# A graph network's second layer: where the split between gathered tiles and weighed blocks stands

## The reference, cut to what matters

```python
def _gcn_conv(x, edge_index, edge_weight, W, b):
    deg = segment_sum(w, col);  dinv = rsqrt(deg)
    norm = dinv[row] * w * dinv[col]
    h = x @ W
    msg = h[row] * norm[:, None]
    return segment_sum(msg, col) + b
x = x + relu(_gcn_conv(h, ...))
```

## Time and profile before

| | us |
|---|---|
| median of 3 runs | 1101.44 (1101.41 to 1103.09) |
| the profiled execution | 1098.35 |
| its span, first to last instruction | 1096.6 |
| layer 2's steps on DVE, in the span | 329.6 to 565.2 |
| busy in the span: PE, DVE, POOL, ACT | 928.3, 827.0, 586.4, 449.9 |

### The profile page before, as it was taken

One profiled execution on the slowest core, in us unless ns is written; L12 is line 12 of the kernel. 1 busy time (PEld: TensorE's weight loads), 2 busy tenths in 40 slices (PEclk: granted clock), 3 DMA queues, 4 the chain that ended last, 5 costly groups with the idle time before them and its releaser, 6 DMA issues.

```text
span 1096.6 us, 23929 instructions
## 1 busy us (share of the span) xinstructions
PE 928.3 (85%) x6145; PEld 587.6 (54%) x6145; DVE 827.0 (75%) x2605; ACT 449.9 (41%) x887; POOL 586.4 (53%) x763
## 2 busy tenths in 40 slices
PE   2788888799957868677777968999999999999995
PEld 2465565354535656565563664555555555555553
DVE  8988888743578767778885586768777877777876
ACT  2577777211005444444430143444444344344342
POOL 6534333000016777777740037777777777777770
PEclk9687877799988898999888969999999999999998
DMA  3000000700001111111108036545444454454441
GB/s 65 1 1 0 0 0 0 274 19 1 1 14 37 27 26 27 27 26 27 27 16 264 15 83 169 117 109 107 107 102 108 102 102 107 100 106 107 100 98 39
DMA packets 145112, 72.82 MB, mean 66 GB/s; under 512 B 111917, under 2 KB 136698, under 8 KB 144922
## 3 DMA queue, kind: packets, MB, share of 16 engines
q1 hardware_dynamic: 127224, 54.98, 19.0%
q0 software_dynamic: 16448, 16.88, 8.7%
q10 hardware_dynamic: 1378, 0.22, 0.1%
HBM read 59.66 MB, written 12.35 MB: 66 GB/s over the span
## 4 chain that ended last, share of the span: by engine, by line
PE 36%; POOL 26%; DVE 14%; issue 13%; ACT 4%; DMA 3%; DVEq 2%; ACTq 1%; SPq 0%; POOLq 0%
POOL pair L1208 14%; POOL A L1208 12%; PE seg L1606 12%; PE big L1530 4%; PE seg L1733 4%; ACT A L1343 4%; PE big L1769 3%; PE big L1759 2%; DMA A<-table,src_i 2%; PE seg L1780 2%; PE seg L1801 2%; PE seg L1544 2%; DVE acc_mem L2086 1%; PE big L1587 1%; PE seg L1790 1%
## 5 line engine op out<-in xcount | busy, mean ns | idle before, releaser
L1208 POOL DMA_INDIRECT A<-table,src_i x338 | 321.4, 951 | 116.3 <-issue 97.0
L1208 POOL DMA_INDIRECT pair<-table,src_i x176 | 177.0, 1006 | 67.4 <-issue 53.3
L1343 ACT CAST A<-big 128x500 f32 x208 | 125.4, 603 | 48.1 <-PE big L1535 24.9
L1733 PE MATMUL seg<-A 128*128 128x384 f16 (+1 forms) x624 | 120.1, 336 | 10.6 <-DVE A L1960 8.2
L1769 PE MATMUL big<-A 128*128 128x512 f32 x208 | 109.8, 609 | 1.5 <-DMA A<-pr_table 1.5
L1450 ACT ACTIVATE A<-big,A 128x512 f32<-128x512 f32 x104 | 71.5, 688 | 93.3 <-PE big L1770 93.3
L1444 ACT COPY A<-big 128x512 f32<-128x512 f32 x104 | 60.8, 584 | 118.4 <-PE big L1759 118.4
L1733 PEld LDWEIGHTS seg<-A 128*128 128x128 f16 x624 | 57.0, 98 | 89.1 <-issue 35.2
L1636 PE MATMUL big<-A 128*128 128x300 bf16 x480 | 93.9, 343 | 5.4 <-DVE A L1883 4.8
L1397 ACT ACTIVATE pair<-pair,wcol 128x64 f32<-128x64 f32 x176 | 46.8, 336 | 109.9 <-DMA pair<-table,src_i 109.8
L1271 POOL COPY cur<-pair 128x24 bf16 x100 | 39.7, 439 | 95.5 <-PE seg L1544 95.5
(11 more groups left out here) (306 smaller groups left out, 1770.9 us busy)
## 6 DMA issues: line engine op xcount, KB each, us to landing
A<-in_edge_attr_dram SPq DMA_DIRECT2D x103, 128.0 KB
A<-drel_flat SPq DMA_DIRECT2D x104, 126.0 KB
spilled_adjacency<-A SPq DMA_DIRECT2D x1, 7074.0 KB, 21.9
A<-spilled_adjacency SPq DMA_DIRECT2D x6, 1152.0 KB, 11.7
A<-table,src_i POOLq DMA_INDIRECT x338
A<-pr_table SPq DMA_DIRECT2D x104, 31.5 KB
pair<-table,src_i POOLq DMA_INDIRECT x176
A<-low_flat SPq DMA_DIRECT2D x78, 32.0 KB
```

Source lines behind the costliest of these rows:

```text
L1208: pool.indirect_dma_start(out=row, out_offset=None, in_=table, in_offset=bass.IndirectOffsetOnAxis(ap=src_i[:, tile:tile + 1], axis=0)).th ...
L1343: nc.scalar.copy(A[:, :, bass.ds(bases[k], PW)], big[:, k % 4, 0:PC].rearrange("p (s d) -> p s d", d=PW)).then_inc(window_kept, 1)
L1733: op = nc.tensor.matmul(made[:, 0:held.shape[2] * D], hot_low[:, u, m, :], held[:, k, :, :], start=(m == 0 and k == 0), stop=(m == 3 and k ...
```

## The change

One group of 16 tiles moves from the gathered to the weighed kind: `IT1` is 10, so 160 tiles are gathered in 40 groups, and NB becomes 16. The groups are spread over one more block (`sum_step`). The chunks of the two sides divide at chunk 10 in place of 11: the ready chunks of the gathered side are 6 in place of 7, the early chunks begin a block later, the chunks left for the end are 8, 9 and 20 to 24 in place of 8, 9, 10 and 21 to 24, and one scratch place moves.

```diff
-IT1 = 11
+IT1 = 10
-SIDE = 11
-FIRST_EARLY = 4
+SIDE = 10
+FIRST_EARLY = 5
-READY = (7, 8)
+READY = (6, 8)
 def sum_step(g):
-    return g + Q + 3 * Q * g // (Q * IT1 - 1)
+    return g + Q + 5 * Q * g // (Q * IT1 - 1)
...
-        early_at = (8 * 2 * D + G * GW, 19 * 2 * D)
+        early_at = (20 * 2 * D + 3 * G * GW, 19 * 2 * D)
...
-                    conv1_late(0, (9, 10, LATE_STRIDE + 9, LATE_STRIDE + 10, 8))
+                    conv1_late(0, (8, 9, LATE_STRIDE + 8, LATE_STRIDE + 9, LATE_STRIDE + 10))
...
-                    return v[:, 0:2 * LATE_STRIDE].rearrange("p (k c) -> p k c", k=2)[:, :, 9:11]
-                return v[:, 0:2 * LATE_STRIDE, :].rearrange("p (k c) d -> p k c d", k=2)[:, :, 9:11, :]
+                    return v[:, 0:2 * LATE_STRIDE].rearrange("p (k c) -> p k c", k=2)[:, :, 8:10]
+                return v[:, 0:2 * LATE_STRIDE, :].rearrange("p (k c) d -> p k c d", k=2)[:, :, 8:10, :]
...
-            late_nodes(big[:, 0, 4 * D:5 * D].rearrange("p (c d) -> p c d", d=D), lambda v: v[:, 8:9], spare(1))
+            late_nodes(big[:, 0, 4 * D:5 * D].rearrange("p (c d) -> p c d", d=D), lambda v: v[:, LATE_STRIDE + 10:LATE_STRIDE + 11], spare(1))
...
-            split3(slice(7, 8), early_parts[0][:, 7:8, :, :])
+            split3(slice(READY[0], 8), early_parts[0][:, READY[0]:8, :, :])
```

More of the change, by code:

```diff
@@ L861, in dense_path @@
                    for at in (20 * 2 * D, 20 * 2 * D + G * GW, 20 * 2 * D + 2 * G * GW, 8 * 2 * D)]
-        early_at = (8 * 2 * D + G * GW, 19 * 2 * D)
+        early_at = (20 * 2 * D + 3 * G * GW, 19 * 2 * D)
         early_a, early_b = (pair[:, at:at + 2 * D].rearrange("p (k d) -> p k d", k=2) for at in early_at)
-        assert early_at[0] + 2 * D <= SIDE * 2 * D and 20 * 2 * D + 3 * G * GW <= NC * 2 * D
+        assert early_at[0] + 2 * D <= NC * 2 * D and 8 * 2 * D + G * GW <= SIDE * 2 * D and SIDE + READY[1] <= 19
         acc_h = acc_mem[:, :].bitcast(F16)
```

## The result

The changed kernel took 1091.45 us (median of 4, 1089.08 to 1091.64) against 1101.43 before: a ratio of 0.990, 95% interval 0.9881 to 0.992, so -9.98 us. Forecast were -12.5 and 1088.9. The range held it, and the direction, and the two medians lie 1 and 2.5 us short of the forecast.

The account below looks back on a forecast made before the run. POOL's gathers were taken to bound layer 2, with DVE next. The last nine blocks' -12.3, and -0.7 and +0.5 behind them, sum to -12.5 us: 1088.9 from the median 1101.44, range 1085 to 1096, wider 1081 to 1097.5.

Parts of the forecast that it names:

- The bound passes from POOL to DVE: In layer 2's last nine blocks, DVE's own work would end at 551.4, behind the gathers' 544.7.
- The added block is covered in the first part: In layer 2's blocks 0 to 6, DVE's 11.1 us for the added block costs nothing, with 5.7 us of cover.
- own work for blocks 0 to 5 was 70.1 us: DVE's time from 329.6 to 416.5 less 16.8 us of waits, before the added block's 11.1 us.
- The entry itself: DVE's begin of block 7, set by the sum of group 14 as block 6's was before: stays at 416.5.
- The nine blocks behind: Blocks 7 to 15 of layer 2: DVE's own work 134.9 us plus 1.5 of waits, ending 552.9; -12.3 us.
- The tail: Behind layer 2's blocks: -0.7 for lateness of the last groups, +0.5 for longer additions and one more PE product.
- the old lengths: Layer 3's first sums come about 12 us earlier, and everything behind them keeps its length.
- Case 3: PE's order holds DVE in layer 2; all 30.6 us of waits stay: +11.1 - 0.2, 1112.3; chance 0.05.
- case 1: Gathers set the end of layer 2's blocks throughout: -19.5 us, 1082; chance 0.12.
- Case 2 (PE's pace): In layer 2's blocks PE falls behind DVE at low clock, leaving up to 7 us more waits: -5.5, 1096; chance 0.17.
- Case 5: The start check turns to the general path, or something else holds layer 3; no time changes; chance 0.03.
- The rule weighed in the prediction: Busier VectorE starves layer 2's gathers; one more block lengthens them 0.8 us, their saving falling from 20.9 to 20.1.

## Why the prediction was right

- **The bound passes from POOL to DVE: shown.** Gathers left out are worth 10.6 us before and nothing after; DVE work in the late blocks is free before and costs at least its full length after.
- **The added block is covered in the first part: shown,** by the idle work that was free there. Block 7 began at 417.25 (forecast 416.5, alarm at 418). The size was off in both directions: DVE's own work in blocks 0 to 6 was 77.9 us (87.6 less 9.8 of waits), not 81.2, and its waits there 9.8, not 5.7. The step that failed is "own work for blocks 0 to 5 was 70.1 us". It is a slip: the wait of 2.73 us ahead of 416.52 lies behind the window of the earlier trace rows, which ends at 416.4. I took it out of the later blocks and never put it to the earlier ones, so it was counted as work. With it the own work was 67.4 us, plus 11.1 for the block 78.5, and the cover 8.4 us. The forecast didn't hang on it, because it took the entry from group 14.
- **The entry itself is partly luck.** DVE is marked with no wait at 417.25. Its last one, 1.48 us at 410.23, is for step 24, which stands behind group 13. PE summed group 14 at 415.94, 1.4 us later than before (414.51), and would have let DVE in at about the same time.
- **The nine blocks behind:** own work 134.2 us (135.1 less 0.9), forecast 134.9; waits 0.9, forecast 1.5. End 552.34 against 552.9. This term carried the result. The place of the waits was wrong: 0.7 and 0.2 us stand in blocks 7 and 8, none around step 38. My 450.9 for that step doesn't follow from 14.4 us a block either; ten steps behind 416.5 it is 452.5, later than the group's 451.7.
- **The tail:** from the blocks' end to the sums behind the late parts it was 24.25 us before and 24.59 after, +0.3 where I had -0.7 + 0.5. The 0.37 and 0.66 us that I took for lateness of the last groups are there unchanged (0.39 and 0.66), so they were never waits for a gather; that term was wrong by 0.7. To the first late sums the gain was 12.6 us where the sum said 12.5, but as -12.9 and +0.3 in place of -12.3 and -0.2: two errors that cancel.
- **Behind it the old lengths were forecast, and 2.1 to 2.3 us came back:** 1.3 and 1.7 of them at a lower granted clock in the first late sums. With the first trace of the kernel before the spans differ by only 6.8 us (1096.6 and 1089.8), with the second pair by 10.9 (1101.3 and 1090.4): that first execution was the fastest of all of the kernel before, and its layer 4 3.3 us shorter than in the second trace (granted clock 0.98 against 0.97). My shift onto the median dealt with this.
- **Two sums of the rivals were off.** Case 3 carries the same 2.7 us: 67.4 + 11.1 + 134.9 + 30.6 = 244.0, so 8.4 us more than 235.6 and not 11.1. In case 1, 20.1 less 0.5 and 0.5 is 19.1, not 19.5.
- **Case 2 (PE's pace)** had a grain of it, but in another place: PE's clock cost 1.3 to 1.7 us behind the steps, not in them, where it was higher than before and PE's busy time 179.7 us, not 189.4. Case 3 is excluded: with gathers left out the waits from block 6 on fell from 11.1 to 1.0 us in PE's old order. Case 5 is excluded by the time itself.
- **The gathers weren't slowed:** they took 1003 ns in the mean after and 1006 before, at a DVE share of 0.86 and 0.79. The rule weighed in the prediction (the Trainium skill, SBUF — State Buffer, section "Who interferes with whom": a VectorE instruction in a two-port mode blocks GpSimd until it ends) did not decide here; no run shows which of the instructions run in such a mode.

## What to carry to other kernels

When two engines take turns holding a stage, price a shift of work as the smaller of two numbers: what the holder sheds, and how much the next one waits now less what it takes on. Read the slack by parts of the stage, because work is free only where the waits are. A wait for a group that is due too early is moved by its due step, and hardly by having fewer groups; moving one part of the order alone sent the wait to the next here.

## What the hardware showed that I had not expected

The first sums behind the stage run at a granted clock of 0.74 in both traces of the changed kernel and at 1.00 in both of the kernel before. The other traces divide in the same way: 1.00 in the two variants of the kernel before, also in the one with fewer gathers that comes to these sums 12.7 us earlier, and 0.57 to 0.75 in the eight traces of variants built on the changed kernel, the one with 36 groups among them. PE waits about as long for DVE in the 25 us before (9.4 us before, 9.5 after). To L1587 these sums take 6.1 to 8.0 us in the traces of the changed order and 4.7 in the others, so this loss is in the time of every variant of the changed kernel. Why the clock is low in one order and not in the other wasn't tried, and stays open.
